# Moving fourteen input adds of a gated attention and mixture-of-experts kernel from VectorE to GpSimd, with eight PSUM banks for the output projections

## The reference, cut to what matters

```python
x = L0_attn_x                                  # (4, 1024, 256) float32
xn = _layernorm(x, axis=-1)
s = _L0_attn_ref(xn, ...)                      # 16 heads of 16; ends with attn @ o_w.T + o_b
g = _silu(_L0_ffn_ref(xn, ...))                # 8 experts, the best 2 of each token, weighted and summed
x = x + s * g
return x
```

## Time and profile before

| what | value |
|---|---|
| time before, median of 3 runs | 718.47 us (714.88 to 721.5) |
| the profiled execution's own time | 721.25 us |
| its span | 719.4 us |
| mean granted clock of TensorE | 0.983 |
| busy, PE / DVE / ACT / POOL | 681.2 / 535.6 / 484.8 / 236.3 us |
| HBM traffic over the span | 170 GB/s |

### The profile page before, as it was taken

The page is one execution under the profiler, slowest core; times in us unless marked ns, Lnnn a source line. Parts: engine busy times, 40 slices in busy tenths (PEclk is TensorE's granted clock), DMA queues, the critical chain, the costliest instruction groups (busy, mean ns, idle before and its releaser), DMA issues.

```text
span 719.4 us, 17538 instructions
## 1 busy us (share of the span) xinstructions
PE 681.2 (95%) x6042; PEld 460.7 (64%) x6042; DVE 535.6 (74%) x1146; ACT 484.8 (67%) x994; POOL 236.3 (33%) x336
## 2 busy tenths in 40 slices
PE   6994999999999999999999999999789999999985
PEld 4873766555565556556555655654359998999764
DVE  6563887999989999998998999896224554444298
ACT  4551443677877877788787778878776666666374
POOL 5331211234023424323342432300034757566300
PEclk9996999999999999999999999999999999999998
DMA  6899976243765686477568657610369786955396
GB/s 213 267 259 312 330 225 200 79 65 87 106 138 138 136 173 148 124 170 156 137 140 174 140 130 164 166 28 19 89 132 259 255 195 219 233 182 174 121 391 248
DMA packets 74903, 124.46 MB, mean 173 GB/s; under 512 B 14184, under 2 KB 44392, under 8 KB 74696
## 3 DMA queue, kind: packets, MB, share of 16 engines
q1 hardware_dynamic: 65200, 95.17, 51.9%
q0 software_dynamic: 9616, 28.17, 12.7%
HBM read 72.56 MB, written 49.72 MB: 170 GB/s over the span
## 4 chain that ended last, share of the span: by engine, by line
PE 81%; DVE 9%; DMA 4%; issue 3%; ACT 2%; POOL 0%; SPq 0%; POOLq 0%; DVEq 0%; ACTq 0%
PE ps L1588 20%; PE ps L1519 14%; PE ps L1572 13%; PE ps L1676 8%; PE ps L1698 8%; PE ps L1508 7%; PE ps L1468 5%; DVE mxa L1111 3%; PE ps L1478 3%; PE ps L1659 2%; DVE x_room L1425 1%; DVE arena L1420 1%; DMA q_parts<-arena 1%; DVE arena L1410 1%; DMA arena<-xs_dram 1%
## 5 line engine op out<-in xcount | busy, mean ns | idle before, releaser
L1111 DVE TENSOR_REDUCE mxa<-ps 128x1 f32<-128x512 f32 (+3 forms) x608 | 358.3, 655 | 45.4 <-PE ps L1508 30.9
L972 ACT ACTIVATE arena<-ps 128x512 f32<-128x512 f32 x576 | 303.7, 603 | 83.1 <-PE ps L1572 42.9
L1519 PE MATMUL ps<-aug 57*128 57x512 f32 (+3 forms) x768 | 218.6, 403 | 11.7 <-issue 9.1
L1572 PE MATMUL ps<-aug 59*128 59x512 f32 (+3 forms) x768 | 215.3, 398 | 0.5 <-ACT arena L972 0.5
L1588 PE MATMUL ps<-arena,v_q 128*32 128x512 f32 (+3 forms) x1536 | 154.4, 497 | 6.7 <-ACT arena L972 6.3
L1572 PEld LDWEIGHTS ps<-aug 59*128 59x128 f32 x768 | 109.4, 185 | 75.9 <-ACT arena L972 70.3
L1519 PEld LDWEIGHTS ps<-aug 57*128 57x128 f32 x768 | 110.0, 188 | 47.4 <-DVE mxa L1111 24.3
L867 POOL DMA_INDIRECT xs_dram<-arena,slot x64 | 62.6, 978 | 75.6 <-ACT arena L972 71.7
L894 POOL DMA_INDIRECT y_dram<-arena,y_row_of x71 | 69.4, 977 | 52.4 <-DVE y_row_of L1349 45.2
L1508 PE MATMUL ps<-key_mask,key_rows 64*128 64x64 bf16 (+2 forms) x704 | 79.7, 209 | 0.0
L1676 PE MATMUL ps<-arena 128*128 128x128 f32 x568 | 75.2, 275 | 0.0
(11 more groups left out here) (149 smaller groups left out, 642.1 us busy)
## 6 DMA issues: line engine op xcount, KB each, us to landing
aug<-k_parts SPq DMA_DIRECT2D x96, 128.0 KB
aug<-q_parts SPq DMA_DIRECT2D x96, 128.0 KB
arena<-xs_dram SPq DMA_DIRECT2D x71, 128.5 KB, 2.6
k_parts<-arena SPq DMA_DIRECT2D x16, 512.0 KB, 4.7
q_parts<-arena SPq DMA_DIRECT2D x16, 512.0 KB, 5.6
arena<-y_dram SPq DMA_DIRECT2D x16, 512.0 KB, 6.7
xn_dram<-arena SPq DMA_DIRECT2D x8, 512.0 KB, 6.3
a_dram<-arena SPq DMA_DIRECT2D x128, 32.0 KB
```

The source lines that it names most:

```text
L972: nc.scalar.activation(prob_slot(q, i), score_bank(q, i), ACT.Exp).then_inc(exp_done, 1)
L1111: nc.vector.tensor_reduce(dst, src, AX.X, ALU.max).then_inc(piece_used, 1)
L1519: ins = nc.tensor.matmul(banks[:, at_ * width:(at_ + 1) * width], k_aug[n][rows, hp, ib * P:(ib + 1) * P], q_aug[n][rows, hp, lo:lo + widt ...
L1572: ins = nc.tensor.matmul(out_[:, col0:col0 + hi - lo], q_aug[n][rows, h // SIDES_OF_ARRAY, jb * P:(jb + 1) * P], k_aug[n][rows, h // SIDES ...
```

## The change

In the last stage GpSimd does the input adds of pairs 0 to 13 (`ON_POOL` = 14); VectorE keeps those of pairs 14 and 15. GpSimd waits once for `x_all_in` and for each pair for `sg_done`, and counts up `fin_done`; VectorE's two adds count up a new semaphore `last_done`, and SP's stores of the last two pairs wait for that. The output projections use all eight PSUM banks (`DEEP_S` = 8): TensorE waits for product m - 8 in place of m - 4, from pair 8 on. `gsum` and `so` keep four buffers, and product m still waits for `fin_done` of pair m - 4, which GpSimd now counts up.

```diff
+DEEP_S = 8
+ON_POOL = NT // 2 - 2
...
-                sp.wait_ge(fin_done, m + 1)
+                if m < ON_POOL:
+                    sp.wait_ge(fin_done, m + 1)
+                else:
+                    sp.wait_ge(last_done, m + 1 - ON_POOL)
                 sp.dma_start(out_t[:, 2 * m:2 * m + 2, :], x_all[:, 2 * m:2 * m + 2, :]).then_inc(stored, 16)
...
+            pool.wait_ge(x_all_in, 16 * NT // 2)
+            for m in range(ON_POOL):
+                tokens = x_all[:, 2 * m:2 * m + 2, :]
+                pool.wait_ge(sg_done, m + 1)
+                nc.gpsimd.tensor_tensor(tokens, tokens, so[m % DEEP].rearrange("p (t d) -> p t d", d=D),
+                                        ALU.add).then_inc(fin_done, 1)
...
-                nc.vector.tensor_tensor(so[j], bank(j), gsum[j], ALU.mult).then_inc(sg_done, 1)
+                nc.vector.tensor_tensor(so[j], bank(m % DEEP_S), gsum[j], ALU.mult).then_inc(sg_done, 1)
...
-                                        ALU.add).then_inc(fin_done, 1)
+                                        ALU.add).then_inc(last_done, 1)
...
-                add_input(m)
+                if m >= ON_POOL:
+                    add_input(m)
...
+                out_ = bank(m % DEEP_S)
                 pe.wait_ge(a_normed, t + 1)
-                if m >= DEEP:
-                    pe.wait_ge(sg_done, m - DEEP + 1)
-                nc.tensor.matmul(bank(j), before_sb[:, P:2 * P], ob_rows.rearrange("p h d -> p (h d)"),
+                if m >= DEEP_S:
+                    pe.wait_ge(sg_done, m - DEEP_S + 1)
+                nc.tensor.matmul(out_, before_sb[:, P:2 * P], ob_rows.rearrange("p h d -> p (h d)"),
...
-                        ins = nc.tensor.matmul(bank(j)[:, i * D:(i + 1) * D], a_all[:, t, k, tokens],
+                        ins = nc.tensor.matmul(out_[:, i * D:(i + 1) * D], a_all[:, t, k, tokens],
```

More of the change, by code:

```diff
@@ L455, in attention_moe_kernel @@
         gsum_done = sem("gsum_done"); silu_done = sem("silu_done"); sg_done = sem("sg_done")
-        fin_done = sem("fin_done"); stored = sem("stored")
+        fin_done = sem("fin_done"); last_done = sem("last_done"); stored = sem("stored")
         SIDES = [(side, m) for side in range(2) for m in range(KT)]
```

## The result

The changed kernel took 725.24 us (median of 4 runs, 723.94 to 731.61) against 719.26 for the kernel before (4 runs). The two medians stand 0.8% apart; the ratio estimated from all these runs is 1.0119, with a 95% interval of 1.007 to 1.0169. A second series gave 1.0127 (1.008 to 1.0174). The forecast was 724.2.

A forecast was written before the change was run, and what follows sets the result against it. VectorE was taken to bound the last stage. Product 0's add and thirteen spacings of 2.41 put product 14 at 719.8; plus 5.27 the span ends 5.7 later: 718.47 + 5.7 = 724.2, range 711.5 to 729.

The forecast's parts named there:

- the beat: Last stage, time from one product on VectorE to the next: 1.99 us before, forecast 2.41 after the change.
- the beat could hardly fall below 1.95: Last stage: with VectorE out of the way, TensorE's 1.95 us for a pair would hold the product spacing.
- The price of GpSimd's add: Each 128x512 input add moved to GpSimd, both inputs in SBUF, takes 1.28 us, as L739 did.
- The collision: GpSimd's add and VectorE's second terms each read two SBUF operands and can't run together: 0.42 us more per pair.
- T+2.21: End of GpSimd's add, counted from the start T of that pair's product on VectorE.
- T+2.41: Start of the next product, counted from the start T of the present one; 0.42 us longer than 1.99.
- The choice that no row decided: When the first second-term instruction ends, GpSimd's add, which asked 0.2 us earlier, goes before the second one.
- rival A: VectorE runs both second-term instructions before GpSimd's add: cycle 1.80 us, span -6.2, time 712.3; chance 0.18.
- Rival B: Second terms never collide with GpSimd's adds; VectorE needs 1.39 a pair, DMA sets the end: -6.7, 711.8; chance 0.10.
- C: Each instruction charged in full after the other, or a longer GpSimd add: 2.75 a pair, +10.3, 728.8; chance 0.15.
- D: The SBUF port goes now to one engine, now to the other: time about 718.5; chance 0.05.
- the last 5.27 us: From the start of product 14 to the end of the span, claimed unchanged at 5.27 us.

## Why the prediction was right, and the step that failed

The bound was read rightly: with 4 banks or 8 VectorE set the beat, and the banks were worth 0 (tail 33.2 with either). Two statements beside it were not. That "the beat could hardly fall below 1.95" was wrong for most of the stage: it was 1.81 with the late adds, 1.86 with the split ones and 1.38 for eight products with the scaled output in PSUM, since loads and projections had been worked ahead. And DMA was not below full from 695 (share 1.04 in 699 to 701, 0.86 in 701 to 703); it fell when all loads were through. Neither enters the forecast's sum.

The price of GpSimd's add, 1.28 from L739, was measured at 1.27 wherever nothing was beside it. Product and add do lie beside each other, as L1066 and L739 did.

The collision was right in place and size. From three small collisions the prediction put together GpSimd's end at T+2.21 and the next product at T+2.41; measured were 0.76 + 1.44 = 2.20 and 2.40 to 2.41. From product 0 to product 14 it had 719.8 - 685.82 = 34.0 us, and the changed kernel took 715.12 - 681.18 = 33.9. The choice that no row decided, GpSimd between the two second terms, held; the run with the late add shows that it was decided by who asked first, as assumed, and that rival A was the right price for the other order. Rival B, a multiply-add that does not collide, is excluded by L1422's 1.48, and rivals A, C and D for this kernel by the beat, which was 2.40 to 2.41 from pair to pair. The rule of the Trainium skill ("SBUF — State Buffer", section "Who interferes with whom"), that a DVE instruction with two SBUF inputs contends with a GpSimd instruction that reads SBUF, held for SCALAR_TENSOR_TENSOR too: 1.48 with both tensors in SBUF, 0.47 with one in PSUM.

What failed is the sentence "Pairs 14 and 15 keep their adds on VectorE, so the last 5.27 us are as before". They were 7.58, 2.3 more. The stretch from product 14 to the end had been taken as VectorE, store and a fixed remainder; it held a wait for all engines, and GpSimd's part in it, 7.5 us behind its last instruction, was hidden only because GpSimd had stopped 42 us before the end. The prediction said that behind GpSimd's wait there was "only the next add"; behind the last add was the drain. The drain and its end at 684.9 were in the trace of before. With this term the sum is 5.7 + 2.3 = 8.0 for a measured 7.9, 1.1%, and on the median that the forecast started from 718.47 + 7.9 = 726.4, just outside the forecast's own 722.9 to 726. That the measured median, 725.24, came within 1.1 us of the 724.2 is therefore in part luck: a term of 2.3 us was missing, and the stages ahead, which were 4.6 us shorter in the profiled execution than before, move the total by more than that. The chance of 0.62 for "within 1%" was too high, since the sum with the drain lies just beyond, as both measured ratios do.

## What to carry to other kernels

Before moving an elementwise instruction to GpSimd, list for each of its instructions the VectorE instructions that can fall beside it and how many operands each reads from SBUF: in this kernel two and two excluded each other, and the way out is to put one operand into PSUM or to let the moved instruction come due beside one that reads PSUM. Where they must meet, who asks first decides, so a small delay or a split of the moved instruction can be worth more than its own time (here 7 us of tail or more for either). Look at where each engine's last instruction stands: an engine given late work brings its closing drain with it, here 7.5 us for GpSimd. The last few instructions are better left where they were: in the version with PSUM, the drain showed with two of the sixteen adds left on VectorE and was covered with four.

## What the runs showed of the hardware that was not expected

GpSimd's closing drain ended 7.5 us after its last instruction in every trace of this document, whether that was an indirect DMA, an add of 512 or of 256 columns, or a one-column memset. The drains of ScalarE and VectorE ended less than 0.1 us after their last instructions. What GpSimd does in it stays open; whether it depends on the indirect DMAs of the stages before was not tried.

More work on an engine made the stage shorter: two memsets of 0.26 us ahead of each of 14 adds took 0.59 us off each beat. And a wait list can name the wrong engine: the 2.4 us at the end stand under TensorE's sequencer, which had been done for 21 us.
